# One read moved behind a piece of the down projection, and the first two turns of a pipelined attention and FFN layer written out

## The chip, the cores and the metric

The kernel runs on one core of a Trainium2 chip. The metric is the device time of one launch in microseconds (us), and lower is better. The profile shows the five engines of the core: PE (TensorE, matmuls; PEld are its weight loads), DVE (VectorE), ACT (ScalarE), POOL (GpSimd) and SP (SyncE, which here issues all DMAs). L378 is line 378 of the kernel before.

## The reference, cut to what matters

```python
def step(carry, inp):                       # one segment of 128 tokens
    mem, z = carry
    q_s, k_s, v_s = inp
    sq = jax.nn.elu(q_s) + 1.0
    att_mem = sq @ mem / (sq @ z)           # read the memory before it is updated
    sk = jax.nn.elu(k_s) + 1.0
    mem = mem + jnp.einsum('bhlk,bhlv->bhkv', sk, v_s)
    z = z + sk.sum(axis=-2, keepdims=True).transpose(0, 1, 3, 2)
    att_dot = softmax(einsum('bhik,bhjk->bhij', q_s, k_s) * scale) @ v_s
    return ((mem, z), gate * att_mem + (1.0 - gate) * att_dot)
...
x = layernorm(x + attention(x) @ Wo)
h = relu(x @ quantize(W1).T + b1)           # quantize: weights become -1, 0 or 1
x = layernorm(x + h @ quantize(W2).T + b2)
```

The input is 8 sequences of 1024 tokens with 512 features, there are 8 heads of width 64, and the FFN has 2048 hidden features. The two FFN weights are divided by the mean of their magnitudes, rounded and clipped.

## The kernel before, in words

The tokens are worked on in 32 groups (`NG`). A group is one segment of 128 tokens of two sequences (`TG` = 2, index `t`), and two pairs of sequences take turns (`LIVE` = 2), so that group g reads the memory that group g-2 has updated. Every fp16 operand of the attention is kept as a high and a low part, so that a product is three matmuls.

Each engine has one list of instructions, written out by a loop `for g in range(NG + 2)`. A pass of it is called a turn here. Turn g does the attention of group g, the output projection, memory update and first layernorm of group g-1, and the FFN of group g-2. A function called with a group outside 0 to 31 issues nothing. Semaphores tie the engines together; the order inside an engine is that of its list.

On PE a turn holds: pieces 1 to 7 of the up projection of g-2 (`ffn_up`, 16 matmuls each) with the q and k projections of g between them (`project_qk`, 24 matmuls each), the output projection (`project_out`), `update_memory`, `scores`, the down projection of the first half of the tokens (`ffn_down(g - 2, 0, 0..3)`, 4 pieces of 8 matmuls), `project_v`, `read_memory(g, 0)` and `(g, 1)`, the down projection of the second half, `attend(g, 0)` and `(g, 1)`, and piece 0 of the up projection of g-1. Six PSUM banks matter here. Banks 2 to 5 are handed out in rotation by `take`, sixteen times a turn, so a job always has the same bank. `read_memory(g, 0)` takes the two banks in which the scores of t = 1 stood and waits until both have been turned into probabilities, that is until `p_lo(g, 1, 1)` on DVE (L751). Banks 0 and 1 serve the up projection in turn.

The softmax runs over DVE and ACT. For a half (t, half) DVE takes the row maxima (`score_max`, L737 and L742), ACT does four exponentials (`exponentials`, L1137) and the high part (`p_hi`, L1148), and DVE the low part (`p_lo`, L751). SP then transposes the probabilities by DMA (`turn_p`). For the scale of the next group's input, DVE takes a maximum (`group_max`, L621), SP sends it to DRAM (`bounce_out`, L1508) and back to all partitions (`bounce_back`, L1515, behind `turn_p(g, 1)`), and DVE goes on from there (`all_max`, L634, then `x_scale`), after which ACT and DVE make the next input (`xt_hi`, L1092, and `xt_lo`).

Turns 0 and 1 have no FFN yet. Between their steps stands the preparation of the FFN weights: `w_sum` and `threshold` find the mean magnitude, `round_w` (DVE, L920) rounds one of eight parts, `turn_w(n)` (PE, L280, four transposes) turns one of 32 blocks, and `put_w(n)` (ACT, L1218) takes its sign out of PSUM. The first 16 blocks use banks 0 and 1, the later ones also 6 and 7. `ffn_up(0, 0)` needs `put_w` of block 28. The scale of the hidden layer comes from the bias (`turn_bias`, `ffn_scale` on DVE, `turn_bias_max`, `spread_bias_max` on PE).

Of the kernel before, what the change touches and what calls it, by code (L numbers as in the profile page):

```python
# [40 lines left out]
def build_program(nc, x, Wq, Wk, Wv, betas, Wo, W1, b1, W2, b2, out):  # L41
# [14 lines left out]
    with ctx:  # L56
# [187 lines left out]
        def _(pe):  # L244
# [278 lines left out]
            for g in range(NG + 2):  # L523
                ffn_up(g - 2, 1)
                if g == 0:
                    turn_max(1)
                ffn_up(g - 2, 2)
                ffn_up(g - 2, 3)
                if g == 0:
                    spread_max(1)  # L530
                if g == 1:
                    for n in range(16, 20):
                        turn_w(n)
                ffn_up(g - 2, 4)
                if g == 1:
                    update_memory(0, 0)
                    update_memory(0, 1)
                project_qk(g, "k", 0)
                if g == 0:
                    turn_max(2)  # L540
                ffn_up(g - 2, 5)
                if g == 0:
                    turn_bias()
                if g == 0:
                    spread_max(2)
# [6 lines left out]
                if g == 0:  # L552
                    turn_max(3)
                ffn_up(g - 2, 7)
                if g == 1:
                    for n in range(20, 24):
                        turn_w(n)
                project_out(g - 1, 0)
                project_out(g - 1, 1)
                if g >= LIVE:  # L560
                    update_memory(g - 1, 0)
                    update_memory(g - 1, 1)
                scores(g, 0)
                scores(g, 1)
                if g == 0:
                    spread_max(3)
# [5 lines left out]
                if g == 0:  # L572
                    turn_bias_max()
                    spread_bias_max()
                if g == 1:
                    for n in range(24, 28):
                        turn_w(n)
# [4 lines left out]
                if g == 0:  # L582
                    sum_all(1)
                ffn_down(g - 2, 1, 1)
                if g == 1:
                    for n in range(28, 32):
                        turn_w(n)
                turn_y(g - 1, 0)
                ffn_down(g - 2, 1, 2)
                if g == 0:  # L590
                    for n in range(0, 4):
                        turn_w(n)
                turn_y(g - 1, 1)
                ffn_down(g - 2, 1, 3)
                if g == 0:
                    for n in range(4, 8):
                        turn_w(n)
                    sum_all(2)
                attend(g, 0)
                if g == 0:  # L600
                    for n in range(8, 12):
                        turn_w(n)
                    for n in range(12, 16):
                        turn_w(n)
# [4 lines left out]
        def _(dve):  # L609
# [312 lines left out]
            def ffn_scale():  # L922
# [3 lines left out]
                dve.tensor_reduce(w(B1_MAX), b1_col[:], AX_X, ALU.max, apply_absolute_value=True).then_inc(sem["bias_max"], 1)  # L926
                dve.wait_ge(sem["bias_row"], 1)
                dve.tensor_reduce(ws[0:1, B1_ALL:B1_ALL + 1], banks[6][0:1, 2 * P:3 * P], AX_X, ALU.max).then_inc(sem["bias_cell"], 1)
                dve.wait_ge(sem["bias_all"], 1)
# [44 lines left out]
            for g in range(NG + 2):  # L974
                if g == 0:
                    w_split("q", 0)
                if g == 1:
                    mem_add(0, 1)
                qk_split(g, "k", 0)
                h_split(g - 2, 4)  # L980
                if g == 0:
                    w_split("q", 1)
                h_split(g - 2, 5)
                qk_split(g, "k", 1)
                if g == 0:
                    w_max("o")
# [4 lines left out]
                if g == 0:  # L991
                    w_split("v", 0)
                    w_chain("o")
                qk_split(g, "q", 1)
                if g == 0:
                    w_split("v", 1)
                residual(g - 1, 0, 0)
                residual(g - 1, 1, 0)
                if g == 0:
                    w_scale("o")  # L1000
# [5 lines left out]
                if g == 0:  # L1006
                    gates()
                group_max(g + 1)
                p_lo(g, 0, 0)
# [3 lines left out]
                if g >= LIVE:  # L1013
                    mem_add(g - 1, 0)
                    mem_add(g - 1, 1)
# [3 lines left out]
                if g == 0:  # L1019
                    w_sum(2)  # L1020
                    ffn_scale()
# [3 lines left out]
                if g == 0:  # L1025
                    w_sum(3)
                invert_sums(g, 0)
                if g == 0:
                    threshold(1)
# [4 lines left out]
                if g == 0:  # L1034
                    round_w(0)
                    round_w(1)
# [3 lines left out]
                if g == 0:  # L1040
                    round_w(2)
                if g == 0:
                    round_w(3)
# [5 lines left out]
                if g == 0:  # L1049
                    threshold(2)  # L1050
# [4 lines left out]
                if g == 0:  # L1055
                    round_w(4)
# [7 lines left out]
                if g == 0:  # L1064
                    mem_add(0, 0)
                if g == 0:
                    round_w(5)
                    round_w(6)
                    round_w(7)
# [5 lines left out]
                if g == 0:  # L1075
                    scalars(0, 3)
# [5 lines left out]
        def _(act):  # L1082
# [147 lines left out]
            for g in range(NG + 2):  # L1230
                if g == 0:
                    w_sum(1, 1)
# [9 lines left out]
                if g == 0:  # L1242
                    w_split("v", 0)
                qk_split(g, "q", 0)
                if g == 0:
                    gates()
# [3 lines left out]
                if g == 0:  # L1250
                    w_split("v", 1)
                qk_split(g, "q", 1)
                if g == 0:
                    w_sum(1, 3)
                    w_sum(1, 0)
                    w_split("o", 0)
                    w_sum(1, 2)
                h_relu(g - 2, 7)
                if g == 1:
                    for n in range(20, 24):  # L1260
                        put_w(n)
# [7 lines left out]
                if g == 0:  # L1269
                    w_split("o", 1)  # L1270
# [5 lines left out]
                if g == 1:  # L1276
                    for n in range(24, 28):
                        put_w(n)
                v_split(g, 1)
                if g == 0:  # L1280
                    w_sum(2, 0)
                    w_sum(2, 1)
                    for n in range(0, 4):
                        put_w(n)
                if g - 1 in EDGES:
                    yt_hi(g - 1, 0)
                if g == 0:
                    for n in range(4, 12):
                        put_w(n)
                if g - 1 in EDGES:  # L1290
                    yt_hi(g - 1, 1)
                if g == 1:
                    for n in range(28, 32):
                        put_w(n)
                xt_hi(g + 1, 0)
                if g == 0:
                    for n in range(12, 16):
                        put_w(n)
# [4 lines left out]
                if g == 0:  # L1303
                    for n in range(16, 20):
                        put_w(n)
# [137 lines left out]
        def _(sp):  # L1443
# [129 lines left out]
            for g in range(NG + 2):  # L1573
                if g == 1:
                    load_ffn_w(2, 3)
                load_blocks(g + 1)
                if g == 0:
                    load_ffn_w(2, 0)
                bounce_out(g + 1)
                if g == 0:  # L1580
                    gates_out()
# [12 lines left out]
                if g == 0:  # L1594
                    load_x(1)
# [32 lines left out]
```

## Time and profile before

| | before |
|---|---|
| median of 3 runs | 1892.02 us (1891.51 to 1892.17) |
| profiled execution, its time | 1893.2 us |
| profiled execution, its span | 1891.4 us |
| PE busy | 1801.1 us, 95% of the span |
| DVE busy | 1424.0 us, 75% |
| ACT busy | 998.7 us, 53% |
| POOL busy | 783.1 us, 41% |
| mean granted TensorE clock | 0.982 of full |
| waits of PE for L378, the memory read | 34.7 us in 30 waits |

The span goes from the first to the last instruction. The 1.8 us between the span and the time of the same execution lie outside the instructions. Busy shares of PE are an upper reading, because matmuls overlap.

### The profile page before, as it was taken

What the parts mean: (1) busy time and instruction counts of PE and PEld (TensorE: products, weight loads), DVE (VectorE), ACT (ScalarE), POOL (GpSimd) and SP (SyncE); (2) the same over time, 40 slices, a digit from 0 to 9 for tenths busy, and PEclk for the clock granted to TensorE, in tenths of its full rate; (3) what the DMA queues carried; (4) which work ended last, traced back from release to release, by engine and by line L of the source; (5) the groups of instructions that cost most, each with busy time, mean ns of one, the idle gap of its engine ahead of it and who ended that gap; (6) DMA issues with size and microseconds to landing.
All of it is one profiled execution on the core that took longest, in us unless ns stands there. A gap on an engine that the chain in (4) does not pass through costs nothing.

```text
span 1891.4 us, 42414 instructions
## 1 busy us (share of the span) xinstructions
PE 1801.1 (95%) x15935; PEld 1254.6 (66%) x15935; DVE 1424.0 (75%) x2807; ACT 998.7 (53%) x2422; POOL 783.1 (41%) x775
## 2 busy tenths in 40 slices
PE   4689999999999999999999999999999999999998
PEld 3466777666677666677766677766677766667765
DVE  6667777878777777877777877777877777877774
ACT  5665645545654555554555554554564554565441
POOL 0203444533454444344444344443344443344442
PEclk9789999999999999999999999999999999999999
DMA  8524335445425355434445434435433434442220
GB/s 273 141 42 75 74 69 87 57 86 87 84 58 92 55 83 91 84 66 81 69 70 92 85 63 82 76 63 92 85 74 70 84 57 88 88 82 59 58 46 23
DMA packets 555130, 150.87 MB, mean 80 GB/s; under 512 B 528544, under 2 KB 532528, under 8 KB 554416
## 3 DMA queue, kind: packets, MB, share of 16 engines
q1 hardware_dynamic: 554928, 148.16, 41.6%
q8 instruction: 129, 2.11, 0.5%
q14 instruction: 73, 0.60, 0.2%
HBM read 50.54 MB, written 16.80 MB: 36 GB/s over the span
## 4 chain that ended last, share of the span: by engine, by line
PE 69%; ACT 16%; DVE 10%; issue 4%; DMA 1%; POOL 0%; SPq 0%; ACTq 0%; DVEq 0%; POOLq 0%
ACT bank L1137 12%; PE bank L448 12%; PE bank L449 11%; PE bank L464 7%; PE bank L465 7%; PE bank L294 6%; PE bank L295 6%; PE bank L296 6%; PE bank L378 3%; PE bank L428 3%; PE bank L426 3%; PE bank L427 3%; ACT y_rows L1175 2%; DVE exp_bias L742 2%; ACT p_rows L1148 1%
## 5 line engine op out<-in xcount | busy, mean ns | idle before, releaser
L448 PE MATMUL bank<-yt,w1t 128*128 128x256 f16 x2048 | 455.5, 273 | 1.9 <-DVE yt L825 1.9
L449 PE MATMUL bank<-yt,w1t 128*128 128x256 f16 x2048 | 455.5, 273 | 0.0
L464 PE MATMUL bank<-w2t,arena 128*128 128x512 f16 x1024 | 395.8, 387 | 0.0
L465 PE MATMUL bank<-w2t,arena 128*128 128x512 f16 x1024 | 395.2, 386 | 0.0
L1193 ACT ACTIVATE arena<-bank,b_scaled,wscalars 128x256 f32<-128x256 f32 x512 | 261.9, 565 | 242.9 <-PE bank L449 171.8
L1137 ACT ACTIVATE bank<-bank,exp_bias,gscalars 128x128 f32<-128x128 f32 x512 | 220.6, 431 | 225.3 <-DVE exp_bias L742 225.3
L448 PEld LDWEIGHTS bank<-yt,w1t 128*128 128x128 f16 x2048 | 200.8, 98 | 25.4 <-ACT w2t L1218 2.0
L449 PEld LDWEIGHTS bank<-yt,w1t 128*128 128x128 f16 x2048 | 200.9, 98 | 23.3
L865 DVE CAST arena<-arena 128x512 f16<-128x512 f32 x256 | 186.7, 730 | 7.8 <-ACT arena L1193 7.8
L1403 POOL TENSOR_TENSOR arena<-arena 128x512 f16<-128x512 f32 x128 | 155.5, 1215 | 76.3 <-DVE arena L865 76.3
L464 PEld LDWEIGHTS bank<-w2t,arena 128*128 128x128 f16 x1024 | 101.6, 99 | 123.0 <-issue 7.7
L465 PEld LDWEIGHTS bank<-w2t,arena 128*128 128x128 f16 x1024 | 101.7, 99 | 117.8 <-issue 7.9
L1325 POOL TENSOR_TENSOR att_mem<-att_mem,gate_in 128x512 f32<-128x512 f32 x60 | 76.3, 1271 | 239.3 <-DVE att_mem L781 239.3
L1092 ACT ACTIVATE xt<-x_blocks,gscalars 128x512 f16<-128x512 f32 x62 | 44.6, 720 | 207.3 <-DVE gscalars L651 207.3
L1347 POOL TENSOR_SCALAR var_eps<-mean_var 128x1 f32<-128x1 f32 x64 | 14.8, 231 | 320.1 <-DVE mean_var L846 320.1
L692 DVE SCALAR_TENSOR_TENSOR xt<-x_blocks,gscalars,xt 128x512 f16<-128x512 f32 x62 | 55.7, 898 | 119.7 <-ACT xt L1092 119.7
L751 DVE SCALAR_TENSOR_TENSOR p_rows<-bank,p_rows 128x512 f16<-128x512 f32 x128 | 88.3, 690 | 72.5 <-ACT p_rows L1148 72.5
L295 PE MATMUL bank<-xt,wk_hi 128*128 128x256 f16 x512 | 140.7, 275 | 0.0
L296 PE MATMUL bank<-xt,wk_lo 128*128 128x256 f16 x512 | 140.7, 275 | 0.0
L294 PE MATMUL bank<-xt,wk_hi 128*128 128x256 f16 x512 | 140.7, 275 | 0.0
L294 PE MATMUL bank<-xt,wq_hi 128*128 128x256 f16 x512 | 139.6, 273 | 0.0
L296 PE MATMUL bank<-xt,wq_lo 128*128 128x256 f16 x512 | 139.6, 273 | 0.0
(180 smaller groups left out, 4317.8 us busy)
## 6 DMA issues: line engine op xcount, KB each, us to landing
rows<-in_L_attn_x SPq DMA_DIRECT2D x32, 512.0 KB, 3.8
out_rows<-rows SPq DMA_DIRECT2D x64, 256.0 KB, 2.4
x_blocks<-in_L_attn_x SPq DMA_DIRECT2D x248, 64.0 KB, 3.0
sk<-sk_t SPq DMA_DIRECT2D x480, 32.0 KB, 2.0
arena<-in_L_ffn_W SPq DMA_DIRECT2D x6, 1024.0 KB, 5.5
w2t<-in_L_ffn_W SPq DMA_DIRECT2D x2, 1024.0 KB, 13.4
w1t<-in_L_ffn_W SPq DMA_DIRECT2D x2, 1024.0 KB, 14.2
amax_row<-amax_dram SPq DMA_DIRECT2D x31, 64.0 KB, 3.5
```

The costliest lines, as they stand in the source:

```text
L294: pe.matmul(ps[:, :, c], w_hi[n][:, k, cols], xt[:, :, k], start=k == 0, stop=False)
L295: pe.matmul(ps[:, :, c], w_hi[n][:, k, cols], xt[:, :, KT + k], start=False, stop=False)
L296: ins = pe.matmul(ps[:, :, c], w_lo[n][:, k, cols], xt[:, :, k], start=False, stop=k == KT - 1)
L448: pe.matmul(ps[:, c], w1t[:, k, cols], yt[:, g % 2, :, k], start=k == 0, stop=False)
L449: ins = pe.matmul(ps[:, c], w1t[:, k, cols], yt[:, g % 2, :, KT + k], start=False, stop=k == KT - 1)
L464: pe.matmul(banks[own][:], h_hi[:, f, toks], w2t[:, f, :], start=f == 0, stop=False)
L465: ins = pe.matmul(banks[own][:], h_lo[:, f, toks], w2t[:, f, :], start=False, stop=f == FT - 1)
L751: dve.scalar_tensor_tensor(out=p_rows[:, t, 1, hs], in0=ps, scalar=2.0 ** 13, in1=p_rows[:, t, 0, hs], op0=ALU.mult, op1=ALU.subtract).the ...
L865: dve.tensor_copy(hi, h32[:, n % NH32]).then_inc(sem["h_hi"], 1)
L1137: ins = act.activation(ps[:, c], ps[:, c], ACT.Exp, scale=gcol(g, G_EXP), bias=exp_bias[:, t, at:at + 1], accum_out=row_sum[:, t, h:h + 1])
L1193: ins = act.activation(h32[:, n % NH32, c * GT:(c + 1) * GT], ps[:, c], ACT.Relu, scale=w(H_SCALE_Y), bias=b1_scaled[:, f:f + 1])
L1403: pool.tensor_tensor(lo, h32[:, n % NH32], hi, ALU.subtract).then_inc(sem["h_pool"], 1)
```

## The change

On PE, in the loop, the first piece of the second half of the down projection comes ahead of the two memory reads. On DVE, in the loop, `p_lo(g, 0, 0)` comes ahead of `group_max(g + 1)`. Turns 0 and 1 are taken out of the loops of PE, DVE, ACT and SP and written out in another order; POOL's list is as it was. In them the values of group 0 follow its scores directly, the blocks of the weights stand between the steps of group 1, ACT puts four blocks between the two halves of group 1's exponentials, and PE starts the up projection of group 0 (`ffn_up(0, 0)` to `(0, 4)`) ahead of `attend(1, 0)` and `attend(1, 1)`. `ffn_scale` is cut in three functions with the same instructions.

```diff
             # PE, the list of turns 0 and 1 (excerpt)
+            scores(0, 0)
+            scores(0, 1)
+            spread_max(3)
+            sum_all(1)
+            project_v(0, 0)
+            project_v(0, 1)
+            for n in range(0, 4):
+                turn_w(n)
+            attend(0, 0)
+            for n in range(4, 8):
+                turn_w(n)
+            turn_bias_max()
+            attend(0, 1)
+            spread_bias_max()
+            project_qk(1, "k", 0)
+            for n in range(8, 12):
+                turn_w(n)
+            sum_all(2)
+            turn_att(0, 0)
+            project_qk(1, "k", 1)
+            for n in range(12, 16):
+                turn_w(n)
+            project_qk(1, "q", 0)
+            turn_att(0, 1)
+            project_qk(1, "q", 1)
+            for n in range(16, 20):
+                turn_w(n)
+            project_out(0, 0)
+            project_out(0, 1)
+            for n in range(20, 24):
+                turn_w(n)
+            update_memory(0, 0)
+            update_memory(0, 1)
+            scores(1, 0)
+            scores(1, 1)
+            for n in range(24, 28):
+                turn_w(n)
+            turn_y(0, 0)
+            turn_y(0, 1)
+            project_v(1, 0)
+            project_v(1, 1)
+            for n in range(28, 32):
+                turn_w(n)
+            ffn_up(0, 0)
+            for g in range(2, NG + 2):
                 ffn_up(g - 2, 1)
                 ffn_up(g - 2, 2)
                 ffn_up(g - 2, 3)
                 ffn_up(g - 2, 4)
+                if g == LIVE:
+                    attend(1, 0)
+                    attend(1, 1)
                 project_qk(g, "k", 0)
...
                 project_v(g, 1)
+                ffn_down(g - 2, 1, 0)
                 read_memory(g, 0)
                 read_memory(g, 1)
-                ffn_down(g - 2, 1, 0)
                 ffn_down(g - 2, 1, 1)
...
             # DVE, turn 0 (excerpt)
+            gates()
+            group_max(1)
+            threshold(1)
+            p_lo(0, 0, 0)
+            score_max(0, 1, 0)
+            w_sum(2)
+            p_lo(0, 0, 1)
+            score_max(0, 1, 1)
+            w_sum(3)
+            p_lo(0, 1, 0)
+            round_w(0)
+            p_lo(0, 1, 1)
+            turn_sk(0)
+            v_split(0, 0)
+            v_split(0, 1)
...
+            xt_lo(1, 0)
+            att_scale(0, 0)
+            xt_lo(1, 1)
+            round_w(2)
+            att_scale(0, 1)
+            bias_maximum()
...
             # DVE, the loop
+                p_lo(g, 0, 0)
                 group_max(g + 1)
-                p_lo(g, 0, 0)
                 score_max(g, 1, 0)
...
             # ACT, turn 1 (excerpt)
+            for n in range(16, 24):
+                put_w(n)
+            exponentials(1, 0, 0)
+            p_hi(1, 0, 0)
+            exponentials(1, 0, 1)
+            p_hi(1, 0, 1)
+            yt_hi(0, 0)
+            yt_hi(0, 1)
+            for n in range(24, 28):
+                put_w(n)
+            exponentials(1, 1, 0)
+            p_hi(1, 1, 0)
+            exponentials(1, 1, 1)
+            p_hi(1, 1, 1)
+            v_split(1, 0)
+            v_split(1, 1)
+            for n in range(28, 32):
+                put_w(n)
+            xt_hi(2, 0)
+            xt_hi(2, 1)
+            h_relu(0, 0)
...
             # SP, turn 1 (excerpt)
+            load_blocks(2)
+            load_ffn_w(2, 3)
+            bounce_out(2)
+            turn_p(1, 0)
+            turn_p(1, 1)
+            bounce_back(2)
+            move_sk(1)
+            turn_att(1, 0)
+            turn_att(1, 1)
+            load_x(3)
```

## Rows read from the trace of the kernel before

**Rows 1.** Waits of PE: engine, line <- releaser: total us, times, longest us

```profile
PE bank L378 <- DVE p_rows L751: 34.7, 30, 1.8
PE bank L308 <- DVE p_rows L751: 11.1, 2, 6.5
PE bank L448 <- DVE yt L825: 1.9, 1, 1.9
```

**Rows 2.** Busy time of each engine in two stretches, with clock and DMA

```profile
91.31:142.33 51.02, 44.34 (x388) 33.51 (x385) 34.45 (x77) 33.53 (x79) 5.17 (x7) 0.90 0.30 50
142.33:198.23 55.90, 54.77 (x498) 38.35 (x496) 37.95 (x74) 30.11 (x74) 21.89 (x22) 1.00 0.39 68
```

**Rows 3.** Timeline of PE, one steady turn: start us, us, instruction [idle before]

```profile
1006.60 0.38 PE L428 MATMUL bank<-wo_hi,at 128*128 128x512 f16 x1
1006.90 1.15 PE L413 MATMUL bank<-v,sk 128*64 128x65 f32 x32
...
1021.10 0.38 PE L309 MATMUL bank<-wv_lo,xt 128*128 128x512 f16 x1
1021.32 0.38 PE L310 MATMUL bank<-wv_hi,xt 128*128 128x512 f16 x1
1022.83 2.00 PE L378 MATMUL bank<-mem,sq_t 64*128 64x65 f32 x32 [1.13 <-DVE p_rows L751]
```

**Rows 4.** Timeline of DVE in the steady turn from 198.23 us

```profile
225.06 1.21 DVE L621 TENSOR_REDUCE amax<-x_blocks 128x1 f32<-128x1024 f32 x1
226.19 0.68 DVE L751 SCALAR_TENSOR_TENSOR p_rows<-bank,p_rows 128x512 f16<-128x512 f32 x1
226.78 0.68 DVE L737 TENSOR_REDUCE row_max<-bank 128x4 f32<-128x512 f32 x1
227.60 0.23 DVE L742 TENSOR_SCALAR exp_bias<-row_max,gscalars 128x4 f32<-128x4 f32 x1
...
234.35 0.69 DVE L751 SCALAR_TENSOR_TENSOR p_rows<-bank,p_rows 128x512 f16<-128x512 f32 x1 [0.55 <-ACT p_rows L1148]
...
242.48 0.28 DVE L634 TENSOR_REDUCE gscalars<-amax_row 128x1 f32<-128x128 f32 x1
```

**Rows 5.** Timeline of ACT, the same turn

```profile
225.34 0.60 ACT L1148 ACTIVATE p_rows<-bank 128x512 f16<-128x512 f32 x1
...
228.28 1.14 ACT L1175 ACTIVATE y_rows<-rows 128x512 f16<-128x512 f32 x2
```

**Rows 6.** Timeline of SP, the same turn

```profile
226.30 0.33 SPq L1508 DMA_DIRECT2D amax_dram<-amax  x1
...
237.19 0.83 SPq L1515 DMA_DIRECT2D amax_row<-amax_dram  x1
```

**Rows 7.** DMA issues from 222 to 280 us: KB, median us to landing

```profile
amax_dram<-amax SPq DMA_DIRECT2D x1, 0.5 KB, 7.7
```

**Rows 8.** Busy time and clock: projection `k`, halves 0 and 1 of group 0

```profile
20.84:26.15 5.31, 5.31 (x26) 3.58 (x25) 2.48 (x7) 4.08 (x4) 0.00 (x0) 1.00 1.05 387
27.56:30.36 2.80, 2.80 (x25) 2.28 (x25) 2.59 (x12) 1.27 (x2) 0.00 (x0) 1.00 0.54 197
```

**Rows 9.** Busy time and clock of stretches of turns 0 to 2

```profile
81.97:90.30 8.33, 7.25 (x80) 5.89 (x78) 4.15 (x7) 7.41 (x14) 2.18 (x2) 1.00 0.85 293
132.00:135.40 3.40, 3.40 (x17) 2.45 (x17) 1.66 (x3) 0.27 (x1) 2.94 (x2) 0.51 0.27 44
```

**Rows 10.** Timeline of PE: two blocks of the weights turned

```profile
81.97 1.07 PE L280 MATMUL bank<-ident,arena 128*128 128x128 f32 x8
```

**Rows 11.** Timeline of ACT, turn 1: first exponential, four blocks put

```profile
112.65 0.43 ACT L1137 ACTIVATE bank<-bank,exp_bias,gscalars 128x128 f32<-128x128 f32 x1 [5.21 <-DVE exp_bias L742]
...
123.50 2.44 ACT L1218 ACTIVATE w2t<-bank,unround 128x512 f16<-128x512 f32 x4
```

**Rows 12.** Timeline of DVE, turn 1: the last `p_lo`, the maximum come back

```profile
122.59 0.69 DVE L751 SCALAR_TENSOR_TENSOR p_rows<-bank,p_rows 128x512 f16<-128x512 f32 x1 [0.55 <-ACT p_rows L1148]
...
129.68 0.29 DVE L634 TENSOR_REDUCE gscalars<-amax_row 128x1 f32<-128x128 f32 x1 [1.10 <-DMA amax_row<-amax_dram]
```

More of the change, by code:

```diff
@@ L973, in _ @@
             scalars(0, 2)
[L974 to L978, printed above, removed]
+            w_split("q", 0)
+            qk_split(0, "k", 0)
+            w_split("q", 1)
+            qk_split(0, "k", 1)
+            w_max("o")
+            qk_split(0, "q", 0)
+            w_split("v", 0)
+            w_chain("o")
+            qk_split(0, "q", 1)
+            w_split("v", 1)
+            w_scale("o")
@@ new lines, in _ @@
+            score_max(0, 0, 0)
+            score_max(0, 0, 1)
+            gates()
[13 more added lines that the diff above has]
+            v_split(0, 1)
+            invert_sums(0, 0)
+            invert_sums(0, 1)
@@ new lines, in _ @@
+            all_max(1)
+            x_scale(1, 0)
+            turn_x(1, 0)
+            x_scale(1, 1)
+            turn_x(1, 1)
+            x_scale(1, 2)
+            x_scale(1, 3)
+            round_w(1)
+            scale_sums(0, 0)
+            scale_sums(0, 1)
+            bias_columns()
+            xt_lo(1, 0)
[4 more added lines that the diff above has]
+            bias_maximum()
+            scalars(1, 0)
+            scalars(1, 1)
@@ new lines, in _ @@
+            round_w(3)
+            ffn_scale()
+            scalars(1, 2)
+            scalars(0, 3)
+            scalars(1, 3)
+            qk_split(1, "k", 0)
+            threshold(2)
+            at_lo(0, 0)
+            round_w(4)
+            qk_split(1, "k", 1)
+            round_w(5)
+            qk_split(1, "q", 0)
+            at_lo(0, 1)
+            qk_split(1, "q", 1)
+            round_w(6)
+            residual(0, 0, 0)
+            residual(0, 1, 0)
+            group_max(2)
+            mem_add(0, 0)
@@ new lines, in _ @@
+            mem_add(0, 1)
+            score_max(1, 0, 0)
+            score_max(1, 0, 1)
+            normalise(0, 0, 0)
+            normalise(0, 1, 0)
+            p_lo(1, 0, 0)
+            score_max(1, 1, 0)
+            p_lo(1, 0, 1)
+            score_max(1, 1, 1)
+            yt_lo(0, 0)
+            round_w(7)
+            yt_lo(0, 1)
+            p_lo(1, 1, 0)
+            turn_x(2, 0)
+            turn_x(2, 1)
+            p_lo(1, 1, 1)
+            v_split(1, 0)
+            turn_sk(1)
@@ new lines, in _ @@
+            v_split(1, 1)
+            invert_sums(1, 0)
+            invert_sums(1, 1)
+            scale_sums(1, 0)
+            scale_sums(1, 1)
+            all_max(2)
+            x_scale(2, 0)
+            x_scale(2, 1)
+            x_scale(2, 2)
+            x_scale(2, 3)
+            xt_lo(2, 0)
+            xt_lo(2, 1)
+            h_split(0, 0)
+            scalars(2, 0)
+            h_split(0, 1)
+            scalars(2, 1)
+            h_split(0, 2)
+            scalars(2, 2)
+            scalars(2, 3)
```

232 lines of the change are left out of this document (83 added, 149 removed).

## The prediction

> **What bounds the kernel now.** I read the page's shares first, then the waits of PE, then the busy time by stretches, then one turn on every engine. PE is busy for 95% of the span. Its longest sum of waits is one line, the memory read L378, 34.7 us in 30 waits for DVE's `p_lo` [rows 1]; turns 2 to 31 have one read each. A steady turn lasts 55.90 us and PE is busy for 54.77 of it [rows 2]; the missing 1.13 us is the wait ahead of the read [rows 3]. So in the loop PE is the bound, with one hole. Turns 0 and 1 are another regime: of the 51 us from the first projection of group 1 to that of group 2, PE is busy for 44.3, at a mean clock of 0.90 [rows 2], and it waits ahead of the values (L308) for 11.1 us and ahead of the up projection (L448) for 1.9 [rows 1].
>
> **The loop: the read behind one piece.** The read needs the last `p_lo` of the turn, which runs from 234.35 to 235.04 [rows 4]. That chain starts at the scores, on PE, and the piece moved does not touch it: piece 0 of the second half needs only hidden features that the first half has used already. The piece is 8 matmuls, and these come 0.215 us apart [rows 3], so it takes 1.72 us, against a hole of 1.13. After it PE comes to the read about 0.6 us after the last `p_lo`. By starts the hole is a little larger: from L310 at 1021.32 the next slot is at 1021.54, the read starts at 1022.83, which is 1.29 us; where PE goes over to the same kind of fp32 matmul without a wait (L428 to L413, 1006.60 to 1006.90) the slot is 0.08 over. So a turn gains 1.21 us. 29 turns give 35.1 us. The longest wait, 1.8 us [rows 1], is taken to be that of turn 31, and of it the piece covers 1.72. Sum 36.8 us.
>
> **Who is late next in the loop.** The read ends 0.6 us later against the DVE chain than now. DVE's first instruction on it does not wait now, since it has `v_split` ahead of it; the maximum L634 at 242.48 [rows 4] follows a run without waits. I put this at nothing; if the 0.6 came through whole, DVE would begin `att_scale` that much later, and PE would not wait for it before the projections of the next turn.
>
> **The loop: `p_lo(g, 0, 0)` ahead of `group_max`.** DVE takes 1.13 us for the maximum, from 225.06 to 226.19, and `p_lo` follows [rows 4]. Its input from ACT is ready at 225.94 [rows 5], so in the new order DVE idles until about 226.0, does `p_lo` to 226.6, and the maximum ends at 227.8 instead of 226.27. `score_max(g, 1, 0)`, queued behind, moves from 226.78 to 227.7, and its bias from 227.83 to 228.75. Who waits for it: ACT's third set of exponentials, but ACT is busy with `yt_hi` until 228.28 + 1.14 = 229.42 [rows 5]. So 0.7 us of cover is left and the last `p_lo` stays where it is. If the cover were gone, every us would move the read's release, of which the piece takes the first 0.6. The other one who waits is SP: the maximum is sent at 226.30 [rows 6], lands 7.7 us later [rows 7], and would now be sent at 227.9 and land at 235.6; SP fetches it back at 237.19 anyway, behind the transpose of the probabilities [rows 6]. 1.6 us of cover: cost nothing.
>
> **Turns 0 and 1.** The same instructions are issued, so what counts is the places of waits. I follow the new lists with the durations of before.
> (a) Group 0's second values no longer stand behind the bias work; they end near 57, not 65. Block 0 can turn at 58.6, when DVE has rounded part 0. Two blocks take 1.07 us at full clock [rows 10] and twice that at the half; a put takes 0.61 [rows 11]. PE turns blocks 0 to 7 and does `attend(0, 0)` until about 69.5.
> (b) A new wait: `spread_bias_max` needs `bias_maximum`, which DVE has behind `xt_lo(1, 1)`, `round_w(2)` and `att_scale(0, 1)`, about 74. Queued behind it on PE is the first projection of group 1. It starts near 74.3, 17 us before the 91.31 of now [rows 2], with 12 blocks (6.4 us) and the memory update (1.1) not done that are done there now: 9.5 us ahead.
> (c) That projection takes 2.8 us at full clock and 5.3 at the half [rows 8]; I take its end at 78.0. From here projections and blocks alternate with ACT: after a projection ACT splits for 1.9 us, then puts; PE turns two blocks, waits 1.4 us for a bank, turns two more. Three such rounds, `turn_att`, the output projections (5.4), four blocks, update and scores bring the scores of group 1 to about 106.6, and DVE's maxima and bias the first exponential to 107.7 + 0.3 = 108.0, against 112.65 [rows 11]. 4.6 of the 9.5 us are left.
> (d) ACT then has `yt_hi` twice (1.1) and four puts (2.44) [rows 5, 11] between the halves of the exponentials. The last `p_lo` of group 1 ended at 123.28, 10.63 after the first exponential; now 108.0 + 10.6 + 3.5 = 122.1. The fetch of the next input's maximum stands behind its transpose; DVE had it 6.4 us later, with a wait for the DMA [rows 12]: 128.5.
> (e) `x_scale` 1.0, `xt_hi` twice 1.4 and `h_relu(0, 0)` 1.0 make 131.9. The new order hides this behind `ffn_up(0, 0)` and `(0, 1)`, which need blocks 28 and 29, put by 124.8. `ffn_up(0, 2)` needs that `h_relu`. Three pieces (16 matmuls of the shape of rows 8, 1.8 us each) and the two attends (an estimate from the same shape at a quarter of its columns: 1.4) bring the first projection of group 2 to 138.8. It was at 142.33 [rows 2]: 3.5 us gained.
> (f) The clock. A wait of 1.9 us ahead of the up projection [rows 1] was followed by 3.4 us at half clock [rows 9]. The rounds in (c) hold waits of 1.4 us. One such stretch costs 1.7 us; I charge 0.5. Turns 0 and 1 give 3.0 us.
>
> On this the Trainium skill (TensorE: Matmul & The Clock Gate, "Part 4: PE-mode transpose") says that transposes don't count as activity for the clock. In the stretch from 81.97 to 90.30, of which transposes fill the most, the granted clock is 1.00 [rows 9], so the trace does not bear it out; by the page the clock would be low through most of (c), which is the second rival.
>
> **Sum.** 1893.2 - 36.8 - 3.0 = 1853.4 for an execution like the profiled one. That one stands 1.2 above the median of 1892.02, so I predict 1852.2 us.
>
> **The rivals.**
> 1. The head gives more: the rounds in (c) run without ACT's waits and the bias wait in (b) is shorter. The 9.5 us of (b) stay: 1846. Against it: (d) lies behind ACT's list whatever PE does. 0.12.
> 2. The head gives nothing or loses: the clock stays at the half through the rounds, where each projection costs 2.5 us more [rows 8]. Three of them and the blocks eat the 3 us and some more: 1855 to 1860, taken as 1858. For it: PE has waits in each round. Against it: rows 9. 0.14. (The page's rule gives this case.)
> 3. A rest of the read's wait stays. If the 0.9 us by which `score_max(g, 1, 0)` is later came through to the last `p_lo`, 0.3 us would be left in 29 turns: 9 us, 1861. Against it: 0.7 us of cover on ACT. 0.08.
> 4. The hole only moves: another wait of PE, such as that for the transposed probabilities ahead of `attend`, ends last and takes the 1.13 us back, and the change does not do what it says: 1889. No wait of PE but the read's shows in the steady turn [rows 1, 2]. 0.03.
> 5. Slower than before: the round trip of the maximum. It is sent 1.6 us later, closer ahead of the transposes. If it then landed only after them, SP would wait at `bounce_back` with the 16 moves of `sk` and `turn_att` behind it. L634 has no wait now; about 5 us of slack (1.6 on SP and some 3 until `xt_hi` is needed) are left before PE feels it. At 6.4 us of delay a turn would be as long as now; at 8 us the kernel would be 50 us slower, 1940. A trip of 7.7 us would have to double. 0.02.
>
> The forecast itself, 1848 to 1856, has 0.61. A measurement of this kernel tells 0.2%, about 3.8 us, from no change. All cases but 4 and 5 lie far below that bound: faster 0.96, same 0.02, slower 0.02. Range: from rival 1 with a us to spare, 1846, to rival 3, 1861; this leaves out 4, 5 and half of the tails of 1 and 3, about 0.15.
>
> **What the changed profile would show.** The wait of PE for L378 falls from 34.7 us to under 1, and steady turns last 54.7 us. DVE's row L634 still has no DMA wait. The exponentials of t = 1 start where they did against the scores. The first projection of group 2 stands near 138.8, after a wait of PE of about 5 us ahead of `ffn_up(0, 0)` for ACT's puts. The prediction is wrong if L378 keeps a wait in every turn, if a new line shows 30 waits, or if the clock of turns 0 and 1 is well below 0.85.

## The result, and the profile after

The kernel takes **1839.75 us** (median of 4 runs, 1839.53 to 1840.93) against 1891.76 us before (4 runs, 1890.69 to 1892.17). The ratio is 0.9727 with a 95% interval of 0.9710 to 0.9744. So it is 52 us faster, where 39.8 were forecast, and it lies 6.2 us below the lower end of the range.

The kernel before was run again beside each group of experiments: medians of 1892.92 us (19 executions), 1891.98 (13) and 1892.81 (7). The ratios below are to these, with a 95% interval in brackets. Of the 39 executions 38 lie from 1889.1 to 1896.6 us and one took 1920.12, at a granted clock of 0.939 where the others have 0.978 to 0.983; ratios leave out such slow executions.

The profiled execution took 1839.69 us, with a span of 1837.9 us and a mean granted clock of 0.990. Against the profiled execution of before (span 1891.4) that is 53.5 us of span.

The waits of PE, same columns as [rows 1]; the top of the view:

```profile
PE bank L480 <- DVE wscalars L882: 8.3, 3, 6.3
PE bank L308 <- DVE p_rows L761: 7.7, 2, 6.2
...
PE bank L280 <- ACT w1t L1296: 5.2, 4, 1.8
...
PE bank L350 <- DVE p_rows L761: 3.5, 2, 1.8
...
PE bank L448 <- ACT arena L1271: 0.4, 1, 0.4
```

The read L378 is gone from the list, and no line has a wait in every turn. What is left belongs to the first two turns, but for one wait of 0.6 us told below. L350 is new: the transposes `turn_y`, which now wait for `p_lo`.

Busy time by stretches, the columns of [rows 2]: the first steady turn, a later one, and the 51 us ahead of the first:

```profile
136.49:191.19 54.70, 54.70 (x502) 38.36 (x499) 38.99 (x71) 29.17 (x72) 25.29 (x24) 1.00 0.43 71
394.60:449.30 54.70, 54.70 (x500) 38.32 (x496) 44.41 (x87) 29.86 (x74) 24.75 (x24) 1.00 0.51 75
85.50:136.49 50.99, 40.65 (x388) 30.63 (x389) 31.71 (x67) 34.28 (x80) 1.51 (x4) 0.90 0.30 59
```

A turn lasts 54.70 us, 1.20 less than in [rows 2], and PE is busy for all of it. The place of the hole, in PE's timeline of a steady turn [rows 3]:

```profile
390.70 0.38 PE L310 MATMUL bank<-wv_hi,xt 128*128 128x512 f16 x1
390.91 0.38 PE L464 MATMUL bank<-w2t,arena 128*128 128x512 f16 x1
...
392.42 0.38 PE L465 MATMUL bank<-w2t,arena 128*128 128x512 f16 x1
392.73 2.00 PE L378 MATMUL bank<-mem,sq_t 64*128 64x65 f32 x32
394.67 0.39 PE L464 MATMUL bank<-w2t,arena 128*128 128x512 f16 x1
```

Eight down matmuls follow the last of the values in its rhythm of 0.215 us, the read starts without a wait, and piece 1 follows it.

DVE, ACT, SP and the DMA issue, in one turn of after, where [rows 4 to 7] have theirs. DVE has the new order:

```profile
218.92 0.69 DVE L761 SCALAR_TENSOR_TENSOR p_rows<-bank,p_rows 128x512 f16<-128x512 f32 x1 [0.82 <-ACT p_rows L1226]
219.53 1.21 DVE L631 TENSOR_REDUCE amax<-x_blocks 128x1 f32<-128x1024 f32 x1
220.65 0.68 DVE L747 TENSOR_REDUCE row_max<-bank 128x4 f32<-128x512 f32 x1
...
227.29 0.69 DVE L761 SCALAR_TENSOR_TENSOR p_rows<-bank,p_rows 128x512 f16<-128x512 f32 x1 [0.54 <-ACT p_rows L1226]
...
235.42 0.28 DVE L644 TENSOR_REDUCE gscalars<-amax_row 128x1 f32<-128x128 f32 x1
```

ACT at that time, with `yt_hi` ahead of the third set of exponentials:

```profile
221.23 1.14 ACT L1253 ACTIVATE y_rows<-rows 128x512 f16<-128x512 f32 x2
222.27 0.42 ACT L1215 ACTIVATE bank<-bank,exp_bias,gscalars 128x128 f32<-128x128 f32 x1
```

SP, with the maximum sent and fetched back:

```profile
220.76 0.33 SPq L1613 DMA_DIRECT2D amax_dram<-amax  x1
...
232.25 0.53 SPq L1620 DMA_DIRECT2D amax_row<-amax_dram  x1
```

The DMA issue of that maximum, from 215 to 275 us, the columns of [rows 7]:

```profile
amax_dram<-amax SPq DMA_DIRECT2D x1, 0.5 KB, 7.4
```

DVE starts the last `p_lo` as soon as ACT has the high part. ACT goes from `yt_hi` straight into the third set of exponentials, so the later bias (221.47 + 0.23) was in time. The maximum leaves at 220.76 and lands 7.4 us later, at 228.2, while SP fetches it back at 232.25: 4 us of cover. But the fetch itself stands later in the turn than before: 41.1 us behind the turn's first projection (232.25 - 191.19), where it was 39.0 (237.19 - 198.23). DVE is at the maximum (L644) 44.2 us into the turn in both. In the turn shown there is no wait, in others there is:

```profile
L644 DVE TENSOR_REDUCE gscalars<-amax_row x31: 277/286/290, 60.7 to 1712.4; 128x1 f32<-128x128 f32 x31
its engine sat idle before it (us, times) until:
  DMA amax_row<-amax_dram: 13.1, 12
```

DVE waits for the fetch in 12 turns, 2.9 us at the longest, where before it waited in one, turn 1. PE has no wait that follows from it.

**Where the 53.5 us came from.** The waits at the read, and so the shorter turns, give 29 × 1.20 + 1.74 = 36.5. The first projection of group 2 starts at 136.49 in place of 142.33: 5.8. One turn lasts 55.49 us, 0.8 more than the others, with this wait of PE inside `attend`:

```profile
456.05 0.19 PE L392 MATMUL bank<-v_hi,pt 128*128 128x64 f16 x1 [0.62 <-issue]
```

The profile puts it down to issue only, but that matmul reads the transposed probabilities of t = 1, whose DMA landed at 455.9, just ahead of it. The transpose for t = 0 had taken 11.6 us from issue to landing, against 6.4 in the turn shown above; why is open. 36.5 + 5.8 - 0.8 is 41.5, and 12 us are missing. They are in seven turns of the kernel before that last 57.59 us and not 55.90, one turn in four. Busy time and granted clock in one of them, from the start of the clock's fall, and then the stretch behind it:

```profile
405.10:408.50 3.40, 3.40 (x10) 1.22 (x9) 3.11 (x10) 0.00 (x0) 1.27 (x1) 0.50 1.30 129
408.50:464.00 55.50, 54.37 (x496) 38.15 (x494) 41.62 (x81) 29.89 (x74) 23.49 (x23) 1.00 0.41 69
```

PE's timeline of before at that place:

```profile
401.34 0.38 PE L310 MATMUL bank<-wv_hi,xt 128*128 128x512 f16 x1
402.85 2.00 PE L378 MATMUL bank<-mem,sq_t 64*128 64x65 f32 x32 [1.14 <-DVE p_rows L751]
404.79 0.39 PE L464 MATMUL bank<-w2t,arena 128*128 128x512 f16 x1
405.01 0.53 PE L465 MATMUL bank<-w2t,arena 128*128 128x512 f16 x1
405.34 0.63 PE L464 MATMUL bank<-w2t,arena 128*128 128x512 f16 x1
405.76 0.63 PE L465 MATMUL bank<-w2t,arena 128*128 128x512 f16 x1
```

PE idles for 1.14 us, does 32 small fp32 matmuls, and right behind them the clock goes from 2.4 to 1.2 GHz for 3.4 us: the down matmuls come 0.43 us apart and not 0.215. Such a fall costs 1.69 us (57.59 - 55.90), and seven of them 11.8. They stand at 405.1, 630.4, 855.7, 1080.9, 1306.2, 1531.5 and 1756.8 us. After the change no such fall is left between 119.8 us and 1836.8 us, the last us of the span. 36.5 + 11.8 + 5.8 - 0.8 = 53.3 of the 53.5.

### The profile page after: what moved, and what is told of

It is laid out like the page before. It is cut to its first block, busy times and chain, and to the rows that moved or that the text cites. A ratio compares the mean times of both kernels' runs of the same rounds, so it can differ in the third digit from the quotient of the medians.

```text
span 1837.9 us, 42414 instructions
## 1 busy us (share of the span) xinstructions
PE 1783.5 (97%) x15935; PEld 1249.6 (68%) x15935; DVE 1461.5 (80%) x2807; ACT 997.0 (54%) x2422; POOL 781.8 (43%) x775
## 4 chain that ended last, share of the span: by engine, by line
PE 95%; DVE 2%; ACT 2%; issue 1%; POOL 0%; DMA 0%; POOLq 0%; ACTq 0%; DVEq 0%
PE bank L464 12%; PE bank L465 12%; PE bank L448 12%; PE bank L449 12%; PE bank L294 6%; PE bank L295 6%; PE bank L296 6%; PE bank L378 3%; PE bank L426 3%; PE bank L428 3%; PE bank L427 3%; PE bank L308 3%; PE bank L310 3%; PE bank L309 3%; PE bank L413 2%; PE bank L327 1%
## 5 line engine op out<-in xcount | busy, mean ns | idle before, releaser
L464 PE MATMUL bank<-w2t,arena 128*128 128x512 f16 x1024 | 388.7, 380 | 0.0
L465 PE MATMUL bank<-w2t,arena 128*128 128x512 f16 x1024 | 388.1, 379 | 0.0
L702 DVE SCALAR_TENSOR_TENSOR xt<-x_blocks,gscalars,xt 128x512 f16<-128x512 f32 x62 | 67.9, 1096 | 93.0 <-ACT xt L1170 93.0
L1473 POOL TENSOR_TENSOR y_rows<-rows,y_rows 128x512 f16<-128x512 f32 x60 | 68.1, 1156 | 171.6 <-ACT y_rows L1253 171.6
## 6 DMA issues: line engine op xcount, KB each, us to landing
w2t<-in_L_ffn_W SPq DMA_DIRECT2D x2, 1024.0 KB, 13.1
```

The costliest lines, as they stand in the source:

```text
L464: pe.matmul(banks[own][:], h_hi[:, f, toks], w2t[:, f, :], start=f == 0, stop=False)
L465: ins = pe.matmul(banks[own][:], h_lo[:, f, toks], w2t[:, f, :], start=False, stop=f == FT - 1)
```

## The experiments

Three theories stood against each other after the result. H: the falls come from the hole beside the read, and vanish with it. H2: they come from the length of the turn against some rhythm of the chip, so that any other length would have removed them. The third: the new order of turns 0 and 1 gave more than was forecast.

**The parts alone.** `loop_only` is the kernel before with nothing but the new order of the read on PE:

```diff
                 project_v(g, 1)
+                ffn_down(g - 2, 1, 0)
                 read_memory(g, 0)
                 read_memory(g, 1)
-                ffn_down(g - 2, 1, 0)
```

> The kernel before with one edit, on PE: the first piece of the second half of the down projection ahead of the two memory reads. Theory H (the seven falls of the clock in the loop of the kernel before belonged to the idle slot directly ahead of the read): steady turns 54.70 us, no turn of 57.6, a gain of 36.5 for the waits and 11.8 for the falls, 1843.5 us. Theory B (the falls come on their own beat, or with something in turns 0 and 1 or in DVE's order, and went away in the changed kernel for that reason): seven or eight turns are still 1.7 us longer, 1855 us.

It took 1841.21 us (1840.97 to 1844.65), ratio 0.9705 [0.9639, 0.9772] to 1892.92 beside it. All turns from 2 on last 54.70 us and none has a fall.

`head_only` is the changed kernel with the old order of that read and of `p_lo(g, 0, 0)` in the loop, so that only the lists of turns 0 and 1 are new.

> The changed kernel with the loops of PE and DVE in their old order, so that only turns 0 and 1 differ from the kernel before. Read from the two profiles, the first projection of group 2 stands 5.8 us earlier, of which 1.3 us were there before any changed instruction. Theory H: a turn of 55.90 with its slot ahead of the read, and turns of 57.6 every fourth time again, so 1891.8 - 4.5 to 5.8 = 1886 to 1887 us. Theory B with turns 0 and 1 as the cause: no long turns, 1875 us.

It took 1890.65 us (1888.39 to 1892.75, 10 runs), 0.9988 [0.9979, 0.9998]. The read waits 34.7 us again and one turn in four lasts 57.6 us. Seven falls stand behind a read as before, and one more at 1809.8 us, behind the read of turn 31, whose wait is 1.82 us long. So the loop alone gives 51.7 us, and the lists of turns 0 and 1 alone give 2.3 (0.4 to 4.0 by the interval), where 4.5 to 5.8 had been expected. The two don't quite add up to the 52 us: on top of `loop_only` the lists give 1.5 (1841.21 to 1839.75).

**Filling the hole without shortening the turn.** `filled` is the kernel before with five down matmuls done once more ahead of the read, into a bank that the next matmul overwrites:

```diff
+            def ffn_fill(g, count):
...
+                for i in range(count):
+                    part = h_lo if i % 2 else h_hi
+                    pe.matmul(banks[7][:], part[:, i // 2, P:2 * P], w2t[:, i // 2, :], start=i == 0, stop=i == count - 1)
...
+                if LIVE <= g < NG:
+                    ffn_fill(g - 2, 5)
                 read_memory(g, 0)
```

> The kernel before, with five matmuls of the down projection done once more ahead of the memory reads (into bank 7, overwritten by the piece that follows), so that the slot of 1.29 us is filled and no work is moved. Nothing is saved in a turn: 55.9 us. Theory H: no falls, 1891.8 - 11.8 = 1880 us. Theory B, or a theory that falls need a turn of just 55.9 us: the falls stay, 1892 us.

1878.96 us (1878.07 to 1881.21, 10 runs), 0.9916 [0.9885, 0.9946]. PE does more work than before and is 14 us faster. The later turn of `filled`, which in the kernel before has the fall at 405.1:

```profile
398.30:454.20 55.90, 55.84 (x502) 38.84 (x501) 43.58 (x86) 29.88 (x75) 24.77 (x24) 1.00 0.42 73
```

The turn is 55.90 us long, as before, with no fall there or in any other. With the length kept and the hole filled the falls are gone: H2 in its plain form is out, and the price of the falls is 11.8 us by the trace (the rest of the 14 lies in the first two turns, whose times differ between executions, below).

**Less of the piece moved.** `half_piece` and `quarter_piece` are the kernel before with four and with two of the eight matmuls ahead of the read.

```diff
+                ffn_down(g - 2, 1, 0, 0, 4)
                 read_memory(g, 0)
                 read_memory(g, 1)
-                ffn_down(g - 2, 1, 0)
+                ffn_down(g - 2, 1, 0, 4, 8)
```

> The kernel before with half of the piece, four matmuls, moved ahead of the reads (0.86 us of the slot of 1.29). A turn takes 55.04 us, 25.8 us less in all. Theory H with any slot doing it: falls remain in a number set by the new turn length, 1857 to 1866. Theory H with a slot that must be long enough: no falls with 0.43 us left, 1854 us.

1853.49 us (1853.26 to 1855.47), 0.9768 [0.9701, 0.9835]. Turns of 55.04 us with 0.27 us of wait at the read, no falls in the loop.

> The kernel before with two matmuls of the piece moved ahead of the reads (0.43 us), so that 0.86 us of the idle slot are left ahead of the read. A turn takes 55.47 us, 12.9 us less in all. Theory H, a slot beside the read costs the clock once it is long enough: if the limit lies under 0.86 us there are still turns 1.7 us longer (up to one a turn, 1880 to 1925 us), if it lies between 0.86 and 1.29 there are none (1867 us).

1867.02 us (1865.87 to 1867.65), 0.9871 [0.9854, 0.9887]. Turns of 55.46 us, no falls in the loop, though each turn still waits:

```profile
400.20 2.00 PE L378 MATMUL bank<-mem,sq_t 64*128 64x65 f32 x32 [0.69 <-DVE p_rows L752]
```

Two matmuls (0.43 us a turn, 13 us in 30 turns) thus brought 25 us: 13 by the wait and 12 by the clock. In these turns of 55.46 us a hole of 0.69 us at the same place, ahead of the same small matmuls, costs no clock. That the shorter hole is the reason is not shown: the length of the turn has changed too, and the next run shows that this matters.

**More work, the hole kept.** `two_more` is the kernel before with two down matmuls done once more behind the two reads.

> The kernel before with two matmuls of the down projection done once more behind the memory reads (overwritten by the piece that follows): 0.43 us more work in each of 30 turns, the idle slot untouched. By work alone 1892 + 13 = 1905 us. Theory H with the falls set by how a turn's length meets the moment at which the chip decides: the number of falls changes from seven to another one, anything from none (1893) to one in each turn (1942 us). A theory in which the slot fills up some store, so that every fourth slot costs a fall: seven or eight falls again, 1905 us.

It took 1895.19 us in the median, 1.0042 [1.0009, 1.0076], but its executions fall apart: of ten, six lie from 1890.13 to 1895.3, three from 1911.16 to 1914.14 (clock 0.978), and one at 1940.93 (clock 0.962). The profiled one (1895.3) has turns of 56.32 us and one fall, of 6.8 us. Its waits for L378 are 34.2 us. A read of an ordinary turn, the read of turn 31, and the stretch of the fall:

```profile
402.60 2.00 PE L378 MATMUL bank<-mem,sq_t 64*128 64x65 f32 x32 [1.11 <-DVE p_rows L764]
...
1810.62 2.76 PE L378 MATMUL bank<-mem,sq_t 64*128 64x65 f32 x32 [1.81 <-DVE p_rows L764]
1811.60:1818.40 6.80, 6.80 (x31) 3.40 (x29) 5.10 (x16) 0.32 (x1) 2.66 (x4) 0.51 0.41 77
```

29 holes of 1.11 to 1.13 us brought no fall here; the only one stands at the hole of 1.81 us. So this hole does not always bring falls, and a change of the turn's length by 0.42 us, with the hole kept, was enough to remove them in this execution. 0.42 us more work in each turn are 12.6 us in all, and the time rose by 3: in most executions the falls were gone, and in some there were many more. By 1.69 us each, the 22 us from 1890.5 to 1912.3 would be some 13 falls, about one in two turns, and the 50 us up to 1940.93 some 30, one in every turn; both are estimates, since no trace of such an execution was taken.

**A hole at another place.** Three kernels are the changed one with a pause of PE ahead of piece 2 of `ffn_down(g - 2, 0, ...)`, some 10 us ahead of the read and among fp16 matmuls: PE waits for 7, 11 or 16 small memsets of a scratch tile on POOL, one after the other from the end of the scores.

```diff
                 ffn_down(g - 2, 0, 1)
+                if LIVE <= g < NG:
+                    pe.wait_ge(sem["paused"], 11 * (g - LIVE) + 11)
                 ffn_down(g - 2, 0, 2)
...
+                if LIVE <= g < NG:
+                    pool.wait_ge(sem["score"], by_t(g, 1))
+                    for i in range(11):
+                        pool.memset(scratch[:, 0:PAUSE[i]], 0.0).then_inc(sem["paused"], 1)
+                        pool.wait_ge(sem["paused"], 11 * (g - LIVE) + i + 1)
```

> The changed kernel with a pause of PE of about 1.2 us put into each turn between the second and third piece of the first half's down projection, among fp16 matmuls (PE waits there for a chain of seven small memsets on the idle POOL). No idle slot at the read. A turn takes 54.7 + 1.2 = 55.9 us as in the kernel before. Theory H1, an idle slot of this length anywhere can cost the clock: falls again, about 1839.8 + 36 + 12 = 1888 us. Theory H2, it takes the slot and the memory read's small fp32 matmuls together: no falls, 1876 us.

With 7 memsets: 1845.55 us (1845.31 to 1846.4), 0.9759 [0.9745, 0.9774], turns of 54.86. The turn grew by 0.16 us only, where a pause of 1.2 was wanted, and only one turn shows a wait at that place, so this run told nothing of the clock.

> The changed kernel with the pause inside the first half's down projection again, now of eleven memsets on POOL: four more at 0.30 us each as read in the run with seven, where PE's turn grew by only 0.16 us. Pause about 1.37 us, turn 56.1 us; by work alone 1839.8 + 41 = 1881 us. Theory H1 (an idle slot of over 1.1 us anywhere can cost the clock): falls in the loop, 1 to 30 of them at 1.7 us, 1883 to 1930 us. Theory H2 (slot and memory read together): no falls, 1881 us.

With 11: 1876.36 us (1875.94 to 1877.1), 0.9914 [0.9897, 0.9930]. The turns last 55.91 us, as in the kernel before, with this row in each:

```profile
389.41 0.39 PE L466 MATMUL bank<-w2t,arena 128*128 128x512 f16 x1 [1.04 <-POOL scratch L1540]
```

Not one fall in the loop. Against the changed kernel the 36.6 us of the turns are lost and the 11.8 of the clock are kept.

> The same with sixteen memsets: a pause of about 2.9 us among fp16 matmuls in each turn, turn 57.6 us, by work alone 1839.8 + 86 = 1926 us. Under H2 in the form that what counts is how little TensorE does in a stretch, and not the read as such, a pause as long as slot and read were together (3.2 us) brings the falls back: a number of turns of 59.3 us, over 1930 us. If even this has no falls, the read's matmuls are what the clock takes badly.

With 16: 1942.49 us (1941.81 to 1943.07), 1.0264 [1.0249, 1.0279]. The wait is 2.35 us, not the 2.9 expected, and the turns alternate between 57.2 and 58.8 us. PE's timeline in one of the longer turns:

```profile
399.00 0.61 PE L466 MATMUL bank<-w2t,arena 128*128 128x512 f16 x1 [2.35 <-POOL scratch L1540]
```

Busy time and clock in the stretch with the pause, and in the one behind it:

```profile
395.30:398.70 3.40, 1.34 (x7) 0.39 (x4) 2.46 (x5) 3.31 (x15) 2.74 (x12) 1.00 0.01 2
398.70:402.10 3.40, 3.10 (x8) 1.16 (x9) 3.13 (x8) 3.31 (x12) 1.85 (x3) 0.52 0.04 4
```

So the read is not special: a hole among fp16 matmuls brings falls too, here in every second turn, once it is long enough. At nearly equal length (1.04 against 1.13 us, turns equal to 0.01 us) the one ahead of the small fp32 matmuls brought seven and the one among fp16 matmuls none.

**The rest of the change.** `no_plo_swap` is the changed kernel with `group_max(g + 1)` ahead of `p_lo(g, 0, 0)` again:

> The changed kernel with DVE's maximum for the next group ahead of the first low part again, as in the kernel before. Both orders are thought to be hidden behind ACT's list, so 1839.8 us. If the swap had helped, the wait for L378 would come back in part.

1839.73 us (1839.03 to 1840.87), 0.9728 [0.9714, 0.9743]. This part is worth nothing. It is also what brought the waits of L644: here that line waits in one turn, 0.2 us, against 12 turns in the changed kernel.

`attend_first` is the changed kernel with group 1's attention again ahead of the up projection:

```diff
+            attend(1, 0)
+            attend(1, 1)
             ffn_up(0, 0)
```

> The changed kernel with the attention of group 1 ahead of the up projection of group 0 again, instead of behind its first five pieces. In the changed profile PE waits 0.18 us ahead of piece 0 and 0.41 ahead of piece 2, and the transposed probabilities have landed 2 us before piece 0. Theory: the early start of the up projection is worth nothing by itself, 1839.8 to 1840.5 us. Rival: it hides ACT's puts and the next input's scale as its place suggests, 2 to 3 us: 1842 to 1843 us.

1839.46 us (1838.47 to 1840.0), 0.9719 [0.9705, 0.9734]. The up projection begun ahead is worth nothing either.

**A better order of turn 1.** In the changed kernel the transposes of the first layernorm's output (`turn_y(0, t)`) stand ahead of group 1's values and take, in the rotation, the banks in which that group's scores are being turned into probabilities. PE's timeline of after:

```profile
107.46 0.66 PE L350 MATMUL bank<-ident,rows 128*128 128x128 f32 x4 [1.67 <-DVE p_rows L761]
109.91 1.11 PE L350 MATMUL bank<-ident,rows 128*128 128x128 f32 x4 [1.79 <-DVE p_rows L761]
117.19 0.61 PE L308 MATMUL bank<-wv_hi,xt 128*128 128x512 f16 x1 [6.17 <-DVE p_rows L761]
```

The values then wait 6.17 us for the third `p_lo`, which is late itself, because ACT does `yt_hi` and four puts between the halves of the exponentials. They start at 1.2 GHz (0.61 us for one matmul). `values_first` is the changed kernel with the values ahead of `turn_y`, `yt_hi` and `yt_lo` behind the probabilities, and the four puts behind them too:

```diff
             # PE
-            turn_y(0, 0)
-            turn_y(0, 1)
             project_v(1, 0)
             project_v(1, 1)
+            turn_y(0, 0)
+            turn_y(0, 1)
...
             # ACT, between the two halves of exponentials(1, ...)
-            yt_hi(0, 0)
-            yt_hi(0, 1)
-            for n in range(24, 28):
-                put_w(n)
```

> The changed kernel with another order in turn 1: on PE the values of group 1 ahead of the turned rows of group 0, on ACT all four exponentials, then the values, four puts, the rows, four puts, and DVE's low parts to match. In the changed profile PE waits 6.2 us ahead of the values, since the turned rows have taken the two banks whose scores are ready first, and works at half clock after it. Expected: the last low part of the probabilities 3.5 us earlier, with it the next input's scale, and piece 2 of the up projection at 125 instead of 129.8; 3 to 5 us gained, 1835 to 1837 us. Rival: the time comes back as another wait (puts on ACT), 1839.8 us.

**1833.67 us** (1833.28 to 1834.33), 0.9689 [0.9675, 0.9704]: 6 us below the changed kernel and 58 below the one before, more than the 3 to 5 us expected. PE's waits in turn 1 are now these:

```profile
106.61 0.39 PE L308 MATMUL bank<-wv_hi,xt 128*128 128x512 f16 x1 [1.66 <-DVE p_rows L761]
113.95 0.66 PE L350 MATMUL bank<-ident,rows 128*128 128x128 f32 x4 [1.49 <-DVE p_rows L761]
115.94 3.67 PE L280 MATMUL bank<-ident,arena 128*128 128x128 f32 x16 [1.33 <-ACT w2t L1296]
```

4.5 us of waits in place of 9.6, and the first projection of group 2 starts at 130.85, not at 136.49. The lists of PE, ACT and DVE were changed together, so the run doesn't tell how much each gave.

## Why the prediction was right or wrong

**The read behind one piece: right.** 36.8 us forecast, 36.5 measured: 1.20 a turn where 1.21 was worked out, 1.74 in turn 31 where 1.72 was.

**Who is late next: right for PE.** Nobody holds it up. Rivals 3 (1861), 4 (1889) and 5 (1940) did not occur: the read has no rest of its wait, and no new line of PE shows 30 waits. One sign was forecast wrong: DVE's row for the returned maximum was to have no DMA wait, and it waits in 12 turns, 13.1 us in all. The 1.6 us of cover on SP were worked out with the fetch staying where it was in the turn; it came 2.1 us later. PE did not feel it: `p_lo` ahead of the maximum cost nothing, and `no_plo_swap` shows it worth nothing. Of rival 4's kind, a wait for the transposed probabilities, there was one, of 0.6 us.

**The clock in the loop: the step that failed.** The sum counted the wait at the read alone. Step (f) charged the clock for turns 0 and 1 and for nothing else, and the turn of [rows 2] was taken for all of them, although a turn in four was 1.69 us longer. The mean clock of 0.982 was spread over the page's slices so thinly that none of the loop's looked low. The term that lacked is the price of the hole itself: seven falls, 11.8 us. With it the same sum is 1852.2 - 11.8 = 1840.4, against 1839.75 measured. The rows 399 to 410 us of before would have shown it, and so would have adding up the turns: 29 × 55.90 falls short of the span between the same instructions by those 11.8 us.

**Turns 0 and 1: the size right, several steps not.** 3.0 us forecast; `head_only` gives 2.3. The two profiled executions differ by 5.8 us at the first projection of group 2, but that start differs between executions of one order by up to 3.5 us: over the six profiled kernels with the old lists it lies from 138.87 to 142.33, mean 140.5, and over the seven with the new lists (`values_first` apart, `attend_first` among them) from 136.49 to 138.62, mean 137.7. The means differ by 2.7. Step by step, with the forecast first: the wait for the bias ends at 74.3 and 71.3, the first exponential starts at 108.0 and 104.12, the last `p_lo` ends at 122.1 and 119.58, the maximum is taken back at 128.5 and 126.47, the first projection of group 2 starts at 138.8 and 136.49. The waits of PE in the rounds were 1.61 us, twice, where three of 1.4 were forecast. The prediction's last paragraph expected a wait of about 5 us ahead of `ffn_up(0, 0)`; there it is 0.18, and the time stands earlier, in the bank waits of 1.67, 1.79 and 6.17 us, which no step followed. Rival 1 (the head gives 9.5, chance 0.12) was wrong as to where more would come from; `values_first`, with 6 us more, in which ACT's list was eased along with those of PE and DVE, speaks against the reason given, that this list holds whatever PE does. Step (c) reads 5.3 us "at the half" from [rows 8], whose column for the clock has 1.00. The duration supports it all the same: the matmuls there last 0.42 us, as they do from 72.1 to 75.5 us of after, at a granted clock of 0.50, against 0.27 at 1.00.

**Rival 2, the clock of the rounds: did not occur.** From 85.50 to 136.49 the mean clock is 0.90, as in [rows 2] before, and low from 109.6 to 119.8, around the bank waits.

**What is shown and what is not.** Shown: falls of the clock cost the kernel before 11.8 us; filling the hole beside the read removes them at the same length of the turn (`filled`), so that the length alone does not set them; and covering it removes them in the changed kernel. Not shown: that a shorter hole is enough, since in `half_piece` and `quarter_piece` the turn is shorter too. Open: why one turn in four and not each, as the hole is the same 1.13 us in all of them, and why the executions of `two_more` differ. `two_more` speaks for a part of H2: with the hole in place the turn's length matters, 29 holes of 1.12 us without a fall in the profiled execution, and the number differs from execution to execution. So the hole and the length both count: without a hole no loop had falls, and a hole of this size doesn't bring them by itself. That more small fp32 work beside a hole makes it dearer is argued from one pair, 1.04 and 1.13 us, whose lengths are not quite equal.

On short holes the Trainium skill (TensorE: Matmul & The Clock Gate, "A second HAM failure mode: psum-queue depth-cycling") reports a kernel in which PE idles briefly but often between groups of matmuls and its clock swings between the two levels. The trace of before agrees in kind, with one hole of 1.13 us in each turn and seven falls of 3.4 us. The same page's "Why this matters for your kernels" warns only of gaps much longer than that hole, and by that advice alone it would have been harmless; the measurement decides.

## What to carry to other kernels

Price a wait of PE twice: by its length, and by the clock that it may cost. Look for the second by listing the length of every turn, not of one, and by the granted clock in the few us behind the wait; a mean clock of 0.982 hid 11.8 us here. Moving two matmuls into the hole, which left 0.69 us of it, removed the second price here; covering it whole is shown to work at two lengths of the turn, 55.90 us (`filled`) and 54.70. When steps are moved past each other, follow what each takes from a rotation of banks, too.

## What the runs showed of the hardware that was not expected

- In the kernel before, an idle time of PE of 1.13 us ahead of 32 small fp32 matmuls was followed in one turn of four by 3.4 us at 1.2 GHz, 1.69 us lost; one of 0.69 us at that place never was, nor one of 1.04 us among fp16 matmuls; one of 2.35 us there was in every second turn. With turns longer by 0.42 us, the same hole was followed by none in the profiled execution.
- More work made the kernel faster: 5 repeated matmuls in each turn, 1892.92 to 1878.96 us.
- The number of falls can differ between executions of one kernel: `two_more` took from 1890.1 to 1914.1 us in nine of ten executions and 1940.9 in the tenth. The others of this case kept within 0.4% for each kernel, but for one execution of the kernel before, 1920.12 us at a clock of 0.939, of which there is no trace.
